# A graph-attention layer whose softmax weights are written to two places: PSUM for VectorE's products, SBUF for TensorE's denominators

## The reference

```
s_u = x @ W_u.T + b_u ; s_v = x @ W_v.T
e = s_u[src] + s_v[dst] ; e = where(e >= 0, e, 0.2 * e)
m = segment_max(e, dst)
e_exp = exp(e - m[dst])
probs = e_exp / segment_sum(e_exp, dst)[dst]
msg = x.reshape(n, 32, 8)[src] * probs[:, None, :]
out = segment_sum(msg, dst)
x = layernorm(x + out)
```

## Time and profile before

| | |
|---|---|
| median of 3 runs | 4693.43 us (4681.35 to 4693.45) |
| the profiled execution | 4686.26 us, span 4684.5 us |
| POOL busy | 3468.7 us, 74% of the span |
| PE busy | 3095.6 us, 66% |
| DVE busy | 2213.4 us, 47% |
| ACT busy | 908.4 us, 19% |
| granted TensorE clock, mean | 0.814 of full speed |

### The profile page before, as it was taken

One profiled execution on the slowest core, in us unless ns is written; L12 is line 12 of the kernel. 1 busy time (PEld: TensorE's weight loads), 2 busy tenths in 40 slices (PEclk: granted clock), 3 DMA queues, 4 the chain that ended last, 5 costly groups with the idle time before them and its releaser, 6 DMA issues. The chain is left out here.

```text
span 4684.5 us, 61408 instructions
## 1 busy us (share of the span) xinstructions
PE 3095.6 (66%) x13554; PEld 1900.7 (41%) x13555; DVE 2213.4 (47%) x5019; ACT 908.4 (19%) x2810; POOL 3468.7 (74%) x2948
## 2 busy tenths in 40 slices
PE   2548777877777777777777776884545555555541
PEld 1224444444444444444444443552333333443331
DVE  2553333333333333333333332995766667766665
ACT  0212222222222222222222222332000000000002
POOL 4237888888888888888888886775777777777764
PEclk9768888889888888888889897996777767667765
DMA  8667666667666667666667666565443434444431
GB/s 300 168 235 176 125 132 134 133 126 138 129 133 125 133 131 135 124 133 130 135 125 131 133 133 132 177 202 172 115 113 109 113 113 114 114 112 114 114 102 63
DMA packets 471759, 641.52 MB, mean 137 GB/s; under 512 B 173607, under 2 KB 365635, under 8 KB 467886
## 3 DMA queue, kind: packets, MB, share of 16 engines
q0 software_dynamic: 198144, 339.26, 38.1%
q1 hardware_dynamic: 245994, 254.83, 18.2%
q10 hardware_dynamic: 27588, 47.08, 3.1%
HBM read 448.23 MB, written 192.71 MB: 137 GB/s over the span
## 5 line engine op out<-in xcount | busy, mean ns | idle before, releaser
L935 POOL DMA_INDIRECT S<-l_msum,l_sink x784 | 1284.8, 1639 | 254.2 <-issue 213.0
L1466 POOL DMA_INDIRECT l_feats<-X_rows,l_gsrc x880 | 1039.2, 1181 | 326.9 <-issue 264.6
L918 POOL DMA_INDIRECT l_ga<-A_rows,l_gsrc x784 | 789.7, 1007 | 265.6 <-issue 160.0
L1008 PE MATMUL l_psU<-l_hid,l_same 128*128 128x257 f32 x1568 | 585.9, 459 | 535.6 <-ACT l_hid L1044 505.3
L981 PE MATMUL l_psC<-l_table,l_onehot 128*128 x4728 | 727.4, 295 | 0.0
L1532 PE MATMUL l_psU<-l_feats,l_same 128*128 128x264 f32 x1760 | 553.5, 478 | 169.5 <-DVE l_feats L1701 124.6
L1048 ACT COPY l_msum<-l_psU 128x257 f32<-128x257 f32 x784 | 292.6, 373 | 1889.9 <-POOLq L934 1313.6
L974 PE MATMUL l_psC<-W1cT,l_attrT 64*128 64x256 f32 x1576 | 623.4, 479 | 13.0 <-DMA l_table<-B_rows 13.0
L981 PEld LDWEIGHTS l_psC<-l_table,l_onehot 128*128 128x128 bf16 x4728 | 426.1, 104 | 367.9 <-issue 306.0
L1008 PEld LDWEIGHTS l_psU<-l_hid,l_same 128*128 128x128 f32 x1568 | 267.4, 214 | 666.2 <-ACT l_hid L1044 579.0
L1532 PEld LDWEIGHTS l_psU<-l_feats,l_same 128*128 128x128 f32 x1760 | 409.0, 240 | 306.9 <-issue 216.8
(11 more groups left out here) (346 smaller groups left out, 3390.7 us busy)
## 6 DMA issues: line engine op xcount, KB each, us to landing
l_srcb<-src_rows SPq DMA_DIRECT2D x99, 512.0 KB
l_locb<-lo_rows SPq DMA_DIRECT2D x55, 512.0 KB
S<-su_zeros ACTq DMA_DIRECT2D x24, 1156.5 KB
l_locb<-loc_rows SPq DMA_DIRECT2D x99, 256.0 KB
nd_sums<-S SPq DMA_DIRECT2D x196, 128.5 KB, 2.2
l_attr<-in_edge_attr SPq DMA_DIRECT2D x98, 256.0 KB
GH_rows<-l_hidden SPq DMA_DIRECT2D x49, 384.0 KB
nd_hidden<-GH_rows SPq DMA_DIRECT2D x49, 384.0 KB, 3.1
```

The lines of the kernel that those rows point to most:

```text
L918: pool.indirect_dma_start(ga[:, s, :], None, D["A"], bass.IndirectOffsetOnAxis(ap=gsrc[h][:, j % HALF:j % HALF + 1], axis=0)).then_inc(gat ...
L935: pool.indirect_dma_start(D[f"S{j % NTAB}"], bass.IndirectOffsetOnAxis(ap=sink[j // HALF][:, j % HALF:j % HALF + 1], axis=0), msum[:, j % ...
L1008: nc.tensor.matmul(psU[j % 2][:, 0:UW], same[j // HALF][:, j % HALF, :], hid[:, j % RING, :], start=True, stop=True).then_inc(agg_done, 1)
L1466: pool.indirect_dma_start(feats[r][:, t, :], None, D["X1"], bass.IndirectOffsetOnAxis(ap=gsrc[r][:, t:t + 1], axis=0)).then_inc(gathered[r ...
```

## The change

The exponential is taken twice. ACT first writes the 128x128 weights to a PSUM bank of their own, `psW` (the eighth), and signals `weights_ready`; then it takes the same exponential again into `feats` and signals a new semaphore, `weights_in_rows`. DVE waits for the first and reads the weights of its four products from PSUM. PE waits for the second, once a group, ahead of its first sum. The comparison (`find_edge`) stays as it was, with both inputs in SBUF.

```diff
+        psW = m.ps("psW", [P, 512])
...
-        below_ready, weights_ready = m.sem("below_ready"), m.sem("weights_ready")
+        below_ready, weights_ready, weights_in_rows = m.sem("below_ready"), m.sem("weights_ready"), m.sem("weights_in_rows")
...
+        weight = psW[:, 0:GROUP * NH].rearrange("p (t h) -> p t h", h=NH)
...
                 pe.wait_ge(same_ready, g + 1)
+                pe.wait_ge(weights_in_rows, g + 1)
...
-                nc.scalar.activation(feats[r][:, :, H:XW], below[:, :, :], ACT.Exp).then_inc(weights_ready, 1)
+                nc.scalar.activation(weight, below[:, :, :], ACT.Exp).then_inc(weights_ready, 1)
+                nc.scalar.activation(feats[r][:, :, H:XW], below[:, :, :], ACT.Exp).then_inc(weights_in_rows, 1)
...
-                    f = feats[r][:, q * QUARTER:(q + 1) * QUARTER, :]
-                    f3 = f[:, :, 0:H].rearrange("p t (c h) -> p t c h", h=NH)
-                    w3 = f[:, :, H:XW].unsqueeze(2).to_broadcast([P, QUARTER, H // NH, NH])
+                    f3 = feats[r][:, q * QUARTER:(q + 1) * QUARTER, 0:H].rearrange("p t (c h) -> p t c h", h=NH)
+                    w3 = weight[:, q * QUARTER:(q + 1) * QUARTER, :].unsqueeze(2).to_broadcast([P, QUARTER, H // NH, NH])
```

## The result

The changed kernel takes 4926.98 us (median of 4 executions, 4921.57 to 4941.55) against 4693.44 us of the kernel before on the same chip: 1.050 times its time, 95% interval 1.046 to 1.054. The forecast was 4670 us.

A forecast was written before the change was run, and what follows sets the result against it. Layer 1 was taken as bound by POOL in under half its groups, elsewhere by DVE and PE. -32.7 + 13.4 = -19.3 us from 4686.3 gave 4667, by the median 4674; forecast 4670 us, range 4642 to 4695.

The forecast's parts named there:

- The changed instructions: Layer 1's products and exponentials: product duration unchanged at 1222 ns, both exponentials and PE's extra wait covered, cost 0.
- The collisions: POOL's gathers beside products no longer stretched: 1.9 us a group less, mean near 1.06 us; those beside `find_edge` stay stretched.
- The waits for gathers: DVE's 24 waits for gathers ahead of L1589 in layer 1 should all go: -32.7 us.
- the 2 us of the forecast: POOL's loop ahead of that of DVE and PE, so POOL idles for PE's `agg_done` about 2 us a group.
- What comes back: DVE waits longer for PE's sums, 0.56 us in each of 24 groups: +13.4 us, bounds nothing to all of 32.7.
- The sum: Over layer 1, -32.7 + 13.4 = -19.3 us, with the loop of DVE and PE at 23.8 us a group.
- A: Rival: no added DVE wait for PE comes back; -33 us, 4654 us, up to -50 us; chance 0.20.
- B: Rival: DVE's wait for PE almost all returns; 0 to -12 us; 0.28 with the uncollided case and a PSUM start cost.
- C: Rival: the product with weights in PSUM is itself longer; at half the rate +235 us, 4900 us; chance 0.07.
- That the collision isn't lifted: Rival: something other than the second SBUF operand holds the gather; 0 us, called unlikely, its chance within a shared 0.28.
- an estimated 65 ns a product for the PSUM source: Start cost on DVE's products by the skill: 14 us over 220, making the sum -5 instead of -19; not adopted.

The follow-up runs named there:

- e6: The changed kernel, with POOL clearing a small scratch tile and waiting for that behind every 4th gather; 4735.7 us, 1.008 times the kernel before.
- e13: The changed kernel, with POOL clearing a scratch tile and waiting for it behind three of each sixteen gathers; 4685.5 us, 1.005 times the kernel before.
- e8: The changed kernel, with at most four gathers under way, POOL waiting for the one four back; 4976.2 us, 1.058 times the kernel before.
- e9: The changed kernel, with each gather from group 2 on fetching rows of 132 floats instead of 264; 4947.8 us, 1.054 times the kernel before.
- e15: The changed kernel, with POOL issuing plain DMAs of 128 consecutive rows instead of gathers from group 2 on; 4609.8 us, 0.989 times the kernel before.
- e2: The changed kernel, with POOL clearing a scratch tile and waiting for that behind every gather; 5137.8 us, 1.102 times the kernel before.

## Why the prediction was wrong

**The changed instructions.** All these steps were right. L1704 takes 1216 ns (forecast 1222). The exponentials take 281 ns to PSUM and 293 ns to SBUF, and the product starts 0.39 us after the first of them starts, against 0.41 before. PE never waits for ACT: its wait ahead of L1535 is for L1704.

**The collisions.** Right: beside products a gather takes 0.94 to 0.95 us (one of 171 takes more), beside `find_edge` still up to 3.06, and the mean is 1041 ns where I said 1060. What I took from the trace of before, that only two SBUF operands stretch a gather, holds for products and adds. It isn't the whole list: in the trace of before 69 of the 93 gathers that ran beside `find_node`, a `tensor_scalar` with one SBUF tensor, and not beside a product or the comparison, took over 1.0 us, up to 1.37, 12 us in all. Small DVE steps ran beside them too, so which instruction it is isn't shown. The change touches neither.

**The waits for gathers.** Right: the 32.7 us are gone, and POOL idles for PE instead. But it idles 406.0 us there, against 50.7 before, by the own views of the two lines: 6.6 us more a group, not the 2 us of the forecast. The 2 us held for groups of 23.8 us; they grew to 28.9.

**The step that failed** is "What comes back": that by a POOL that is ahead only PE's slow start would return, +13.4 us, at most the 32.7. Measured is 244.1 + 32.7 = 277 us, and it isn't PE's matmuls, which take 482 ns instead of 478. Its bounds held only what is queued behind the removed wait. They didn't ask what else a POOL that issues without being held up does to the engines around it. A gather in an unbroken row starts every 1.25 us, and with such rows PE's signals to DVE, ACT and POOL come late, by up to 11.7 us: 77 of the 127 late ones arrived only after the row's last gather had started. Gathers that DVE stretched to 1.4 and 2.4 us had kept the row slack. So the collision that the change removes had a use; that the slack is what helped is inferred, from the pauses of e6 and e13, which put it back by other means.

The runs order themselves by pitch, wherever it comes from (on several chips, see above): 1.29 us gives a stretch of 1684 us, 1.37 to 1.39 give 1561 to 1634, 1.42 gives 1515, 1.44 and 1.45 give 1439 and 1421, and 1.51 gives 1302 to 1317. Above, at 1.58, it rises again, since POOL is then the bound. Edits of quite different kinds lie on this one line: products, comparison, pauses, rows, bytes, gathers under way. The pitch isn't the whole of it: e8 and e9 have nearly the same one and lie 54 us apart, and at 1.50 to 1.51 us 61, 20 and 55 signals are late.

**The second trace of it, overlooked.** The sum took the groups of before as 23.8 us of real work. In e15, where no signal is late, they take 1239.1/54 = 22.95 us with the same DVE and PE work. On e15's chip the kernel before is 30 us faster, though, which could be 0.56 of the 0.84 us a group between the two. The 61 late updates tell it directly: some late signals were in the 24.4 us as well, the groups of 32.25 and 37.76 us most of all. These two, and rows that say "remote" or name a transfer long done, were the warning in the trace of before.

**The rivals.** A and B are refuted by the same step. C forecast 4900 us, near the result by chance: its mechanism, a product at half the rate, would show as some 2290 ns at L1704, which takes 1216. That the collision isn't lifted is refuted by the gather's mean. The Trainium skill, "VectorE: DVE Perf Modes", section on the TRN2 errata, would add an estimated 65 ns a product for the PSUM source; the trace has 6 ns less than before. The Trainium skill, "SBUF — State Buffer", section "Who interferes with whom", is borne out in that the product stretches the gather with two SBUF operands and leaves it alone with one; its inference that `tensor_tensor` leaves POOL's DMAs alone doesn't hold for indirect ones here.

**What stays open.** Which part the gathers and PE's signals share isn't settled, nor why only PE's signals are affected. Not every signal of PE's in a row is late: in the group shown above, by the timeline DVE idled only 0.42 us for PE at 3802.13, with POOL in the same row, and none of the 34 recorded updates of that semaphore in the kernel after is over 15 ns behind. Nothing here tells what singles out the late ones. Nor was a gather's instruction told apart from the 16 completion signals that each sends, beyond that e15 sends as many. Nor is a part of the recording itself excluded: every execution here carries the profiler's span and clock, and beside indirect gathers records get lost (of DVE's chained steps the trace of the kernel after has 385 updates of 753, e15's has all 753). Lost records alone don't make signals late, since e2 loses some too and has none late. No version was found that beats the kernel before and computes the same.

## What to carry to other kernels

Before freeing an engine that issues indirect gathers, ask how densely it will then issue them and who waits for PE meanwhile; a gap that looks like a loss may be what keeps the signals in time. A pause of about 0.8 us behind every fifth gather is a cheap probe for it, and the pitch of the gathers is the number to plot. In a trace, an engine that waits long after its producer has ended, with a releaser that can't be or "remote", and a few groups far longer than the rest, are where to look first. Then compare the end of the sender's instruction with the start of the one that waited, for each pair of engines: that tells whose signals are late.

## What the runs showed of the hardware

- With indirect gathers of 128 rows at an unbroken pitch of 1.25 us, PE's semaphore updates come up to 11.7 us late (127 of 586 by over 1 us), those of DVE, ACT and POOL at most 12 ns. At a mean pitch of 1.50 to 1.51 us 20 to 61 are late, at 1.58 us one, by 1.6 us. Halving the bytes or the rows or limiting the gathers under way to four doesn't help.
- Plain DMAs issued by POOL with the same packets, in bursts of 16 at 0.53 us, don't do it (0 of 702).
- Gathers beside a DVE `tensor_scalar` of 128x2048 bf16 elements and the small steps around it take up to 1.37 us instead of 0.946.
- A 64-row gather takes 0.90 us, a 128-row one 0.946: nearly all of it is fixed.
- A small POOL instruction between two gathers is hidden (0.11 us, then 0.19 us instead of 0.30); waiting for its result costs 0.8 us.
- A 128x1024 product on DVE takes 1216 ns with its broadcast operand in PSUM and 1222 ns in SBUF; a 128x128 exponential on ACT takes 281 ns into PSUM and 293 ns into SBUF.
